# A two-step mixture of experts around linear attention on one core: where the returned rows are added, where half of the second shared expert runs, and 60 buffers for its rows

## What is computed

```python
x = x + 0.5 * ffn(layernorm(x))
x = x + attention(layernorm(x))      # linear attention, 16 heads, chunks of 128, decay, gate, group norm
x = x + 0.5 * ffn(layernorm(x))

def ffn(x):                          # 32 experts, 6 of them for each token
    combine = softmax(x @ gate.T), 3 best of 8 groups, 6 best experts, renormalized
    for e in experts:                # w1, w3: 256 -> 128, w2: 128 -> 256
        y += combine[:, e] * ((silu(x @ w1[e].T) * (x @ w3[e].T)) @ w2[e].T)
    shared = (silu(x @ sw1.T) * (x @ sw3.T)) @ sw2.T        # 256 wide inside, for every token
    return y + shared
```

## Time and profile before

| | us |
|---|---|
| median of three runs | 956.46 |
| lowest, highest | 954.28, 975.6 |
| profiled execution | 960.5 |
| its span, first to last instruction | 958.7 |

### The profile page before, as it was taken

The page is one execution under the profiler, slowest core; times in us unless marked ns, Lnnn a source line. Parts: engine busy times, 40 slices in busy tenths (PEclk is TensorE's granted clock), DMA queues, the critical chain, the costliest instruction groups (busy, mean ns, idle before and its releaser), DMA issues. The chain is left out here.

```text
span 958.7 us, 16120 instructions
## 1 busy us (share of the span) xinstructions
PE 772.8 (81%) x4554; PEld 609.0 (64%) x4555; DVE 513.0 (54%) x1439; ACT 358.5 (37%) x799; POOL 465.3 (49%) x487
## 2 busy tenths in 40 slices
PE   6895997999969789788889575686999995867486
PEld 6464885888847546576677374564888884645154
DVE  5774942434313537888887469672444431135274
ACT  3160443444424314465665224233444442322000
POOL 3005665553053335867754320655555406456884
PEclk9979898999988898999999755688999998887798
DMA  6862465643233463222220140233444413334524
GB/s 209 338 286 77 158 214 176 231 164 120 89 121 114 159 227 89 80 76 67 72 62 2 34 176 1 77 121 120 153 158 154 138 77 121 126 112 131 207 82 153
DMA packets 42358, 126.43 MB, mean 132 GB/s; under 512 B 8352, under 2 KB 16704, under 8 KB 39488
## 3 DMA queue, kind: packets, MB, share of 16 engines
q1 hardware_dynamic: 23872, 75.40, 20.7%
q0 software_dynamic: 18432, 50.36, 18.0%
HBM read 76.44 MB, written 49.28 MB: 131 GB/s over the span
## 5 line engine op out<-in xcount | busy, mean ns | idle before, releaser
L399 POOL DMA_INDIRECT back<-token_table,slots x192 | 186.7, 973 | 221.9 <-DVE slots L644 96.3
L911 PE MATMUL bank<-w,xt 128*128 x1024 | 260.7, 400 | 33.2 <-ACT xt L492 18.4
L911 PEld LDWEIGHTS bank<-w,xt 128*128 128x128 f32 x1024 | 196.5, 200 | 69.4 <-issue 44.2
L420 POOL DMA_INDIRECT back<-slot_table,combine x124 | 130.0, 1049 | 143.6 <-SPq L328 42.2
L690 DVE TENSOR_TENSOR mids<-mids,bank 128x256 f32<-128x256 f32 x128 | 53.8, 420 | 256.6 <-ACT mids L469 197.3
L931 PE MATMUL bank<-w,mids 128*128 x512 | 142.9, 405 | 4.5 <-DVE mids L697 2.6
L492 ACT COPY xt<-ring 128x256 f32 x256 | 91.5, 408 | 104.0 <-issue 75.9
L931 PEld LDWEIGHTS bank<-w,mids 128*128 128x128 f32 x512 | 93.2, 203 | 16.0 <-issue 7.1
L469 ACT ACTIVATE mids<-bank 128x256 f32<-128x256 f32 x128 | 49.0, 383 | 145.2 <-PE bank L911 87.8
L680 DVE COPY ring<-bank 128x512 f32 (+1 forms) x96 | 66.1, 689 | 46.6 <-PE bank L901 31.2
L923 PE MATMUL bank<-const,mids 128*128 128x128 f32 x256 | 52.6, 290 | 45.7 <-DVE mids L690 24.2
(11 more groups left out here) (209 smaller groups left out, 1070.9 us busy)
## 6 DMA issues: line engine op xcount, KB each, us to landing
slot_table<-gT SPq DMA_DIRECT2D x32, 512.0 KB
slot_table<-ey SPq DMA_DIRECT2D x32, 512.0 KB
w<-in_w SPq DMA_DIRECT2D x12, 1024.0 KB, 17.1
slot_table<-w SPq DMA_DIRECT2D x6, 1024.0 KB
token_table<-back SPq DMA_DIRECT2D x8, 512.0 KB, 2.9
back<-token_table,slots POOLq DMA_INDIRECT x192
x<-in_x SPq DMA_DIRECT2D x4, 512.0 KB, 5.7
turn_a<-in_turn SPq DMA_DIRECT2D x4, 512.0 KB
```

The costliest lines, as they stand in the source:

```text
L399: pool.indirect_dma_start(out=rows[q % RX][:, a * H:(a + 1) * H], out_offset=None, in_=table, in_offset=bass.IndirectOffsetOnAxis(ap=slots ...
L420: pool.indirect_dma_start(out=returned[g % len(returned)], out_offset=None, in_=y_table, in_offset=bass.IndirectOffsetOnAxis(ap=combine[:, ...
L911: last = nc.tensor.matmul(bH[u % 2][:, a * 2 * I:(a + 1) * 2 * I], xt[u % 2][:, a * H + k * P:a * H + (k + 1) * P], w13[:, bass.ds(expert[ ...
```

## The change

1. **f = 1, additions.** None among the tiles any more. All six columns are added behind the tiles: column 0, product, column 1, product, column 2, four shared additions, columns 3, 4, 5.
2. **f = 1, buffers.** 60 instead of 28 (the change's own words say 61; 28 + 18 + 14 are 60, and the first gather that waits for an addition is g = 60). The new ones are the weights of the first six experts (`spared`, 18 rows' room, free when 48 pairs are through) and the dead ends of the ring and a seventh expert's weights (`freed`, 14, free when 56 pairs are through). The weights of those six experts are therefore loaded again at the end of attention.
3. **f = 1, shared expert.** Turns 0 and 1 (half of the tokens) move into the opening, at the same places as in f = 0. Turns 2 and 3 stay behind the tiles; SP reads their tokens back when 56 pairs are up.
4. **f = 0.** Column 0 is added behind the tiles, column 1 in attention: five additions a tile there instead of four (ADDS = 5), the extra one from `spared`. POOL's pacing by `e_h` is gone; it waits once, for 48 pairs, before the first `spared` buffer.

The core of the diff:

```diff
+GONE = 6
 REST = TOPK - EARLY
+ADDS = REST + EARLY - 1
+LASTS = 8
+DEAD = (ST - 2 * LASTS - E + 1) % RR
...
+        spared = [part[:, i * H:(i + 1) * H] for part, n in ((w13, GONE * WE // H), (w2, GONE)) for i in range(n)]
...
-                    returned = [back[:, i * H:(i + 1) * H] for i in range(KEEP)]
+                    freed = [ring[:, a + i * H:a + (i + 1) * H] for a, n in (
+                        (spare + 2 * KC * TB, 2), (SPAN + spare, 6), (0, 4)) for i in range(n)]
+                    freed += [w13[:, GONE * WE + i * H:GONE * WE + (i + 1) * H] for i in range(WE // H)]
+                    returned = [back[:, i * H:(i + 1) * H] for i in range(KEEP)] + spared + freed
...
+                                if g == (KEEP if f else NT):
+                                    pool.wait_ge(e_h, done + GONE * NT // 2)
+                                    pool.wait_ge(e_yp, done + GONE * NT // 2)
+                                if f == 1 and g == KEEP + len(spared):
+                                    pool.wait_ge(e_h, done + NQ - LASTS)
+                                    pool.wait_ge(e_yp, done + NQ - LASTS)
                                 if g >= len(returned):
                                     pool.wait_ge(s_add, g - len(returned) + 1)
-                                if f == 0 and g % 2 == 0:
-                                    pool.wait_ge(e_h, NQ - NT - 3 + g // 2)
...
-                        pairs(NQ - EDGE, EDGE, final=True)
+                        pairs(NQ - 2, 2)
                         copy_mid(NQ - 1, NQ - 1)
-                        if f == 1:
+                        if f == 0:
+                            for i in range(NT):
+                                add_row(0, i, 0, 2 * len(NOW))
+                        else:
...
+                            add_rows(0, 4)
                             product(2)
+                            add_rows(1, 4)
                             product(3)
+                            add_rows(2, 4)
+                            shared_of(4, 8, 3)
+                            for n in range(3, TOPK):
+                                add_rows(n, 8)
...
-                        if f == 0:
-                            shared_in(0, xnT)
+                        shared_in(0)
                         ranks()
-                        if f == 0:
-                            shared_in(1, xnT)
+                        shared_in(1)
                         for i in range(NT):
                             tokens_of_slots(i)
-                            if f == 0 and i in (8, 13):
+                            if i in (8, 13):
                                 results(i // 5 - 1)
...
+                        sp.wait_ge(add_ok, NT * ADDS)
+                        sp.dma_start(w13[:, 0:GONE * WE], w13_in[:, 0:GONE * WE]).then_inc(s_big, 16)
+                        sp.dma_start(w2[:, 0:GONE * H], w2_in[:, 0:GONE * H]).then_inc(s_big, 16)
...
                                 if k == 0:
-                                    dve.wait_ge(back_ok[j % RB], (j // RB + 1) * REST * 16)
+                                    dve.wait_ge(s_early[1], NT * 16)
...
-                            for k in range(REST):
+                            for k in range(ADDS):
                                 at(add_rows(k), j + 4)
```

181 lines of the change are left out of this document (87 added, 94 removed).

## The result

The changed kernel takes 996.33 us (median of 4 runs, 995.32 to 1002.15) beside 956.88 for the kernel before (4 runs). The ratio is 1.043, with a 95% interval of 1.038 to 1.048: slower by 4.3%. The prediction had 975.3 and a range up to 992.0. The profiled execution has a span of 993.8 us, 35.1 more than the 958.7 of before.

What follows compares the result with a forecast made beforehand. POOL's gathers and the shared expert were taken to end the kernel almost together. Terms 11.3 + 1.5 + 3 + 1 + 6 − 4 = +18.8 took the profiled 960.5 to 979.3, or 975.3 on the median; range 952 to 992.

Steps and rivals of the forecast that it cites:

- The cost behind the tiles: Second half step after its last pair: POOL ends within 1 us of before, better order behind it gains; −4 us.
- The opening: Second half step, choice of experts to slots: a shared expert turn delays the one-hot matmuls; +11.3 us.
- tiles of the second half step: Pairs of the second half step: eight more gathers in unbroken runs beside them cost +6 us.
- Eight more at 0.78 is 6: Second half step's tiles: 40.6 us lost over 52 gathers taken as 0.78 us each, for eight more gathers.
- the upper bound: Second half step's tiles: runs of 16, 30 and 14 gathers lose 53.5 us by length, 13 more.
- ACT's wait of 8.68 us: Sign in the profile before: ACT waits until 881.01 for up matmuls said to end nominally at 875.6.
- A fixed start of 7.4 us a run: Second half step's tiles: each unbroken gather run costs its length less 7.4 us.
- long runs: Rival: unbroken gathers hold pairs for their whole length, additions in a row hold POOL; +36, 992 us; chance 0.18.
- The first half step's tiles: Pairs of the first half step: gathers lose their pacing and run 16 and 16 unbroken; +3 us.
- The relief rival: Rival: additions among pairs or something unchanged cause stalls, additions behind the tiles slow POOL little; −1, 955 us; chance 0.27.
- Attention: Between the half steps: DVE gets 16 additions there, only the first tiles should pay; +1 us.
- the block's end: Behind the first half step's tiles: sixteen additions follow DVE's last copy; +1.5 us.

Runs made afterwards that it cites:

- run 16: No follow-up run has this label; the text's "unbroken runs of 16" are 16 gathers that POOL issues in a row in the first half step.
- the paced half step: Changed kernel with spaced second-half-step additions, plus first-half-step gathers waiting two per pair; on a disturbed chip 980.93 us, ratio 1.019 to the kernel before.
- the kernel with spaced additions: Changed kernel, each second-half-step addition behind the tiles waiting for the one ahead; 1005.58 us, ratio 1.045 (disturbed chip); 873.94 us, 0.990 (quiet), to the kernel before.

## Why the prediction was wrong

**What held.** The order on every engine, and six terms of seven to 1 us (the table). The cost behind the tiles (−4, measured −4.3) held as a total, and that is partly luck: POOL's last gather ends 61.4 us behind the last pair product instead of 64.7, so 3.3 us came from POOL, which I had within 1 us of where it was, and only 1.0 from the order behind it (9.3 us from that gather to the end instead of 10.3), where I had 2 to 4.

**The opening: right number, wrong working.** +11.3 came from comparing the two half steps of the same kernel, which is a measurement, and it measured +11.6. The explanation beside it ("10.09 of it has the size of that one turn") falls: with half of the matmuls it costs the same. Silu, product and 128x256 matmuls together account for 5.3 us up to `slots`; the rest isn't shown. The comparison also stopped too early. In the first half step the first pair product comes 21.48 us behind `slots`, in the second 15.13; the change made that 21.45. These 6.3 us stand in the row of the tiles, where the pairs up to the last 16 gave back 6.4. On a quiet chip all four are 15.1 to 15.2.

**The step that failed: tiles of the second half step, +6, measured +21.5.** The step reads "Eight more at 0.78 is 6": I made a price for each gather out of 40.6 us and 52 gathers. It is the run's length that counts. Columns 1 and 2 became one run of 30 through the extra buffers, I had said so, and the upper bound even worked with lengths; yet the sum took the price by count. On the same measure (last 15 gaps, less the 44.8 that they take on a quiet chip) the loss went from 39.7 to 61.4 us. That is 0.76 and 1.02 a gather, so there is no such price, and the paced half step, with 32 gathers for 1 us, shows it directly. The 40.6 itself came out near 39.7 because two errors cancel: my 90.0 us was a rounder window, and my undisturbed 49.4 us was of pairs that still have transposes in, which the last 16 don't. And ACT's wait of 8.68 us was for matmuls that end at 872.82, not 875.6, which is the next pair: a result 8 us late.

**And the bound was too low.** A fixed start of 7.4 us a run gave +13. Measured by the quiet chip's gaps, the runs of before (70 us in four) lose 39.7, a start of 7.6; those of after (20.2, 39.0 and 17.7, 76.9 us in three) lose 61.4, a start of 5.2. So the rival "long runs" had the mechanism in the tiles, undersized. That its sum, +36, meets the measured 35.1 is partly luck: its tiles are 8.5 too low (+13 for 21.5), its end 7.3 too high (+3 for −4.3). I gave it 0.18. What spoke against it in the text was that no longer run had been seen. That is no evidence; a run of 30 was a step beyond the rows, and the price by count hid it. What is not tested: no kernel with 28 buffers, or with the second half step paced, was measured on a disturbed chip, so that its run of 30 costs by its length is carried over from the first half step and from the stalls beside it.

**The first half step's tiles**, +3, measured +4.0, is a sum of things that I didn't separate. The last 15 gaps grew by 6.1 us (65.0 to 71.1) with the two unbroken runs of 16. Against it, the last copy comes 1.3 us sooner behind the last product, without additions between them, and the rest is small. The wait of DVE for its second column, 10.5 us on a quiet chip, goes away too, but in the recorded profile it was only 1.67 us.

**The relief rival** rested on PE's matmuls following each other at 943.53 under gathers. When matmuls are issued doesn't show when their results arrive, but the consumers bear it out: behind the tiles of before all four silus start within 0.04 us of their matmuls' end. The observation was right. What failed was to carry it over to the pairs, where the changed kernel has no additions at all and stalls for longer.

**Attention** (+1, measured +0.6 and +0.7 on a quiet chip) and the block's end (+1.5, +1.3) need no more.

**What none of my steps could see** is that about 73 us of the kernel before, 957 beside 884, were the disturbance. On quiet chips the same change is worth 0.3%, so its verdict is one on unbroken gathers in that condition. What the condition is, what in a gather holds PE's results in it, and why the results behind the tiles of before escape, stays open.

## What to carry to other kernels

When a stall stands beside a long unbroken series on another engine, don't price it by the piece: compare two lengths of the series, and ask what breaks it up now, since a change that removes a break (a wait, a slow instruction, a full buffer) lengthens the series. A wait that looks like a loss of the engine that has it may be the gap through which others live; pacing 32 gathers by two a pair left the first half step's last 15 gaps at 45 us on a quiet chip, and took them from 73.3 to 46.0 on a disturbed one. And a stage of the same program that has the changed order already is the best price of an edit, but it gives a number and not a cause.

## What the hardware showed that I had not expected

- In some runs PE's results reach ACT and DVE late while POOL issues gathers without a break: 20 us at 850.17 in the changed kernel, 24.8 us behind the tiles of the kernel with spaced additions. In others, with the same program and 96 gathers in a row, not at all, and behind the tiles of the kernel before not even in its disturbed run. The records of an undelayed pair's up matmuls are alike in both, 1.89 us; over the last 16 pairs the granted clock is 1.00 in one and 0.73 in the other, where PE stands idle for 10.43 us ahead of 871.59.
- Sixteen additions on DVE without a gap (6.4 us) stretch a gather under them from 0.96 to between 3.3 and 5.2 us, a run of 32 to 9.59. With each waiting for the one ahead (one in 0.58 us instead of 0.40) the gathers under them take 0.96 to 1.22 us, and 96 take 122.9 us instead of 133.0. The Trainium skill, "SBUF — State Buffer", Who interferes with whom, has a DVE instruction with two SBUF inputs contend with a GpSimd instruction that reads SBUF; these additions have two, and a gather reads its indices there. These runs agree, and add what a run does: without a gap between additions the gather waits over several of them.
